# Cross-attention and a top-2 mixture of experts: tile tails in blocks of 32 in place of 64, with copies, a counting product, a table load and the last step moved

## The reference

```python
# x, ctx: (32, 64, 256) float32; attention takes groups of 8 of the 64 rows as heads
x = x + xattn(layernorm(x), ctx, ctx)          # softmax over 256 keys, 8 rows a head
x = x + ffn(layernorm(x), gate, w0, w1, wo)    # 8 experts, 2 of them per token

def ffn(x, gate_kernel, w0_kernel, w1_kernel, wo_kernel):   # EMB 256, MLP 512
    gate_logits = einsum('bsd,de->bse', x, gate_kernel)
    weights, indices = top_k(gate_logits, 2)
    weights = softmax(weights)
    combine = einsum('bsk,bske->bse', weights, one_hot(indices, 8))
    inter = silu(einsum('bsd,edm->bsem', x, w0_kernel)) * einsum('bsd,edm->bsem', x, w1_kernel)
    return einsum('bse,bsem,emd->bsd', combine, inter, wo_kernel)
```

## Time and profile before

| | |
|---|---|
| median of 3 runs | 501.8 us (499.94 to 504.45) |
| the profiled execution | 499.44 us, its span 497.7 us |
| mean granted TensorE clock | 0.928 |
| PE, DVE, ACT, POOL busy | 88%, 57%, 49%, 43% of the span |
| attention, to the last pv product | until about 238 us |
| planning | about 249 to 265 us |
| expert steps | about 268 to 487 us |

### The profile page before, as it was taken

The page is one execution under the profiler, slowest core; times in us unless marked ns, Lnnn a source line. Parts: engine busy times, 40 slices in busy tenths (PEclk is TensorE's granted clock), DMA queues, the critical chain, the costliest instruction groups (busy, mean ns, idle before and its releaser), DMA issues.

```text
span 497.7 us, 10117 instructions
## 1 busy us (share of the span) xinstructions
PE 438.9 (88%) x3288; PEld 225.4 (45%) x3289; DVE 285.8 (57%) x610; ACT 241.5 (49%) x476; POOL 212.1 (43%) x237
## 2 busy tenths in 40 slices
PE   4948998988999988979479999999999999999991
PEld 3412343433443433424234555555656666666650
DVE  7898989898869898866598423242322222222220
ACT  2654888878668879865202233333322222222220
POOL 9564040454554223296403244455463544444222
PEclk9875999999879999986776999999999999999997
DMA  8776569787967762449961022333333322233211
GB/s 242 218 217 168 139 197 221 220 228 212 262 177 200 199 173 87 126 119 393 398 236 42 22 42 43 53 46 50 53 47 50 63 43 42 42 49 50 30 21 21
DMA packets 42341, 65.27 MB, mean 131 GB/s; under 512 B 6330, under 2 KB 32251, under 8 KB 42299
## 3 DMA queue, kind: packets, MB, share of 16 engines
q1 hardware_dynamic: 28570, 38.49, 27.5%
q0 software_dynamic: 11424, 24.12, 20.8%
q10 hardware_dynamic: 2304, 2.10, 1.3%
HBM read 39.79 MB, written 24.58 MB: 129 GB/s over the span
## 4 chain that ended last, share of the span: by engine, by line
PE 52%; issue 19%; POOL 11%; DVE 7%; DMA 3%; ACT 2%; SPq 2%; ACTq 1%; POOLq 0%; DVEq 0%
PE max_ps L1611 22%; PE pv_ps L1633 6%; PE ring_ps L1633 5%; PE pv_ps L1484 3%; PE ring_ps L1570 3%; DVE mx L1001 3%; PE max_ps L1605 3%; PE ring_ps L1467 2%; POOL normed L636 2%; ACT pt L839 2%; PE ring_ps L1560 2%; POOL q_sb L622 2%; POOL num L616 2%; PE ring_ps L1628 2%; SPq L443 1%
## 5 line engine op out<-in xcount | busy, mean ns | idle before, releaser
L1001 DVE TENSOR_REDUCE mx<-max_ps 128x4 f32<-128x1024 f32 x128 | 150.2, 1216 | 19.2 <-PE max_ps L1343 19.1
L839 ACT ACTIVATE pt<-ring_ps 128x512 f32<-128x512 f32 x256 | 139.1, 598 | 32.4 <-PE ring_ps L1467 28.9
L1611 PE MATMUL max_ps<-w_sb,pt 128*128 x256 | 115.4, 593 | 1.0 <-ACT pt L903 0.9
L766 POOL DMA_INDIRECT out<-rb,sidx x36 | 56.8, 1578 | 96.8 <-DVE rb L1319 42.2
L1297 DVE TENSOR_TENSOR pt<-pt,max_ps 128x512 f32<-128x512 f32 x36 | 24.8, 688 | 104.9 <-issue 86.0
L1484 PE MATMUL pv_ps<-pt,w_sb 128*27 128x256 f32 (+2 forms) x1024 | 81.4, 402 | 1.1 <-ACT pt L839 0.5
L1611 PEld LDWEIGHTS max_ps<-w_sb,pt 128*128 128x128 f32 x256 | 46.1, 190 | 47.3 <-issue 47.3
L1467 PE MATMUL ring_ps<-Q,K 50*128 50x256 f16 x512 | 53.2, 288 | 11.6 <-ACT pt L839 8.9
L1343 PE MATMUL max_ps<-K,Q 48*128 48x256 bf16 x512 | 53.4, 289 | 11.0 <-DVE mx L1001 11.0
L910 ACT ACTIVATE pt<-ring_ps 128x512 f32<-128x512 f32 x36 | 21.5, 597 | 68.7 <-PE ring_ps L1570 68.7
L903 ACT ACTIVATE pt<-ring_ps 128x256 f32<-128x256 f32 x36 | 13.8, 384 | 67.1 <-PE ring_ps L1560 44.8
(11 more groups left out here) (216 smaller groups left out, 540.1 us busy)
## 6 DMA issues: line engine op xcount, KB each, us to landing
w_sb<-in_L_ffn_w_kernel POOLq DMA_DIRECT2D x16, 512.0 KB, 10.6
K<-k_img SPq DMA_DIRECT2D x14, 448.0 KB, 6.2
Q<-q_img SPq DMA_DIRECT2D x14, 448.0 KB, 7.7
k_img<-kpart SPq DMA_DIRECT2D x28, 192.0 KB, 3.7
q_img<-qpart SPq DMA_DIRECT2D x28, 192.0 KB, 3.4
wo_sb<-in_L_ffn_wo_kernel POOLq DMA_DIRECT2D x8, 512.0 KB, 12.7
acc<-pvs SPq DMA_DIRECT2D x6, 512.0 KB, 3.1
q_sb<-in_x SPq DMA_DIRECT2D x16, 128.0 KB, 4.1
```

The costliest lines, as they stand in the source:

```text
L766: g.indirect_dma_start(xacc, bass.IndirectOffsetOnAxis(ap=sidx[sl.par][:, 0:1], axis=0), y_sb[sl.par], None, compute_op=ALU.add).then_inc( ...
L839: a.activation(pt[:, (2 * i + h) % PTN, :, :], bank(key)[:, :, :], ACT.Exp, scale=SCALE).then_inc(ring_read, 1)
L1001: v.tensor_reduce(mx[:, t % 2, :, :, p].rearrange("q mt h -> q h mt"), max_ps[n % 2][:, :, :, :], axis=AX.X, op=ALU.max).then_inc(max_read, 1)
L1611: last = nc.tensor.matmul(flat(max_ps[sl.par][:, bank_of]), lhsT=xT[sl.par][:, k * P:(k + 1) * P], rhs=weight(w, e, KC, k), start=(k == 0) ...
```

## The change

`TAILS` becomes (64, 32): GRAIN is 32, PER 4, KINDS 4, NT 34, NMIX 6, and a mixed tile has four blocks and nine copies on each of DVE and ACT. DVE's copies are spread anew: the first w0 block is copied in the step of the mixed tile before, and wo blocks a step sooner. `rank(0)` goes from pair 0 to pair 2 of the last tile. On POOL the first `rsqrt_last` stands ahead of four wo loads. ACT runs a one-column SiLU after the exponential of the gate. In the last step PE puts the output of the tile before between the two halves of `hidden`, and DVE makes its product after scaling. With NT = 34 the loop over plain tiles has no rounds left, so all steps from t = 20 on are written out.

```diff
-    TAILS = (64,)
+    TAILS = (64, 32)
...
-    ranks_at = {(T - 1, 0): 0, (T - 1, 7): 1}
+    ranks_at = {(T - 1, 2): 0, (T - 1, 7): 1}
...
             load_each(load_w0, range(E))
-            load_each(load_wo, range(4, E))
...
             rsqrt_last(0, 2, 1)
+            load_each(load_wo, range(4, E))
             load_each(load_w1, range(3))
...
             a.activation(e2[:, :], gap[:, :], ACT.Exp).then_inc(e2_done, 1)
+            a.activation(mx[:, 0, 0, 0, 0:1], nbias[:, 2:3], ACT.Silu)
...
+            def stage_w0(j, n):
+                e = expert_block(j, n + 1)
+                for k in range(KC):
+                    v.tensor_copy(w0_st[n][:, k, :], w0_sb[:, bass.ds(e * KC + k, 1), :].rearrange("p o f -> p (o f)")
+                                  ).then_inc(w0_copied, 1)
             def stage(sl):
                 n = sl.c % EVERY
+                if sl.peeled and sl.t == 0:
+                    stage_w0(0, 0)
+                if n == EVERY - 1:
+                    if sl.c < AFTER - 1:
+                        stage_w0(sl.j + 1, 0)
+                    return
+                if n + 1 < PER - 1:
+                    stage_w0(sl.j, n + 1)
                 if n < PER - 1:
-                    e = expert_block(sl, n + 1)
-                    for k in range(KC):
-                        v.tensor_copy(w0_st[n][:, k, :], w0_sb[:, bass.ds(e * KC + k, 1), :].rearrange("p o f -> p (o f)")
-                                      ).then_inc(w0_copied, 1)
-                if 0 <= n - 1 < PER - 1:
-                    e = expert_block(sl, n)
-                    v.tensor_copy(wo_st[n - 1][:, 0:FC // 2, :], wo_sb[:, bass.ds(e * FC, FC // 2), :]).then_inc(wo_copied[0], 1)
+                    e = expert_block(sl.j, n + 1)
+                    v.tensor_copy(wo_st[n][:, 0:FC // 2, :], wo_sb[:, bass.ds(e * FC, FC // 2), :]).then_inc(wo_copied[0], 1)
...
+            def multiply(sl):
+                v.wait_ge(sil_done, sl.t + 1)
+                v.wait_ge(h1_full, sl.t + 1)
+                if sl.has(-2):
+                    v.wait_ge(inter_turned, sl.t - 1)
+                v.tensor_tensor(inter[sl.par], sil[sl.par], flat(max_ps[sl.par][:, 1]), ALU.mult).then_inc(inter_done, 1)
...
             def experts(sl):
                 if sl.has(GX):
                     next_gather(sl.at(GX))
-                if sl.has(0):
-                    v.wait_ge(sil_done, sl.t + 1)
-                    v.wait_ge(h1_full, sl.t + 1)
...
-                    v.tensor_tensor(inter[sl.par], sil[sl.par], flat(max_ps[sl.par][:, 1]), ALU.mult).then_inc(inter_done, 1)
+                if sl.has(0) and not (sl.peeled and sl.t == NT - 1):
+                    multiply(sl)
...
+                if sl.peeled and sl.t == NT - 1:
+                    multiply(sl)
                 if not sl.plain and sl.c < AFTER:
                     stage(sl)
...
-            def hidden(sl, e):
+            def hidden(sl, e, halves=(0, 1)):
...
+                if sl.peeled and sl.t == NT - 1:
+                    hidden(sl, e, (0,))
+                    output(sl.at(-1), e_before)
+                    hidden(sl, e, (1,))
+                    return
                 if sl.has(0):
                     hidden(sl, e)
```

More of the change, by code:

```diff
@@ L1251, in next_gather, with expert_block @@
                 v.tensor_copy(gidx[sl.buf][:, :], tokg[:, bass.ds(sl.col, 1)]).then_inc(gidx_done, 1)
-            def expert_block(sl, c):
-                return v.value_load(expert_of[0:1, bass.ds(PER * sl.j + c, 1)])
+            def expert_block(j, c):
+                return v.value_load(expert_of[0:1, bass.ds(PER * j + c, 1)])
+            def stage_w0(j, n):
[3 more added lines that the diff above has]
+                                  ).then_inc(w0_copied, 1)
             def stage(sl):
                 n = sl.c % EVERY
-                if n < PER - 1:
-                    e = expert_block(sl, n + 1)
-                    for k in range(KC):
-                        v.tensor_copy(w0_st[n][:, k, :], w0_sb[:, bass.ds(e * KC + k, 1), :].rearrange("p o f -> p (o f)")
-                                      ).then_inc(w0_copied, 1)
-                if 0 <= n - 1 < PER - 1:
-                    e = expert_block(sl, n)
-                    v.tensor_copy(wo_st[n - 1][:, 0:FC // 2, :], wo_sb[:, bass.ds(e * FC, FC // 2), :]).then_inc(wo_copied[0], 1)
+                if sl.peeled and sl.t == 0:
[6 more added lines that the diff above has]
+                    stage_w0(sl.j, n + 1)
+                if n < PER - 1:
+                    e = expert_block(sl.j, n + 1)
+                    v.tensor_copy(wo_st[n][:, 0:FC // 2, :], wo_sb[:, bass.ds(e * FC, FC // 2), :]).then_inc(wo_copied[0], 1)
             def turned_spares():
@@ L1290, in experts @@
                     next_gather(sl.at(GX))
-                if sl.has(0):
-                    v.wait_ge(sil_done, sl.t + 1)
-                    v.wait_ge(h1_full, sl.t + 1)
-                    if sl.has(-2):
-                        v.wait_ge(inter_turned, sl.t - 1)
-                    v.tensor_tensor(inter[sl.par], sil[sl.par], flat(max_ps[sl.par][:, 1]), ALU.mult).then_inc(inter_done, 1)
+                if sl.has(0) and not (sl.peeled and sl.t == NT - 1):
+                    multiply(sl)
                 if sl.peeled and sl.t == 0:
@@ L1599, in hidden @@
                     pe.wait_ge(w1_copied, (sl.j + 1) * KC * (PER - 1))
-                for w, w_st, bank_of, full in ((w0_sb, w0_st, 0, h0_full), (w1_sb, w1_st, 1, h1_full)):
+                for bank_of in halves:
+                    w, w_st, full = ((w0_sb, w0_st, h0_full), (w1_sb, w1_st, h1_full))[bank_of]
                     if sl.mixed:
```

## The result

The changed kernel takes 487.64 us (median of 4 runs, 486.32 to 488.38) against 502.94 us (4 runs) of the kernel before on the same chip: a ratio of 0.970, 95% interval 0.9645 to 0.9755. The profiled execution took 487.11 us, its span is 485.1 against 497.7. The forecast of 488.5 lies near it, its range holds, and so do most terms of its sum; two terms missed by 0.6 and 0.7 us in opposite directions. One sentence of the forecast was wrong, and it stood beside a term of zero: what I said of the copies.

What follows compares the result with a forecast made beforehand. PE's tile count and time bound the expert stage, with PE stops at attention's end and DVE's planning chain besides. Terms summed to -11.8 us: 487.6 from the profiled time, 490.0 from the median, forecast 488.5, range 484.5 to 494.5.

Steps and rivals of the forecast that it cites:

- Number of tiles: Expert stage: blocks of 32 cut the tiles from 36 to 34, two plain steps of 5.82 us fewer, -11.64 us.
- Mixed tiles: Expert stage: six mixed tiles for four, each 0.66 us over a plain one, column groups side by side; +1.5 us, +1.2 to +3.6.
- Copies: Expert steps: nine copies per group on each of DVE and ACT fit in idle time or behind PE's work, 0 us.
- First step: Start of the expert stage: DVE makes five copies and three register loads for two copies; +0.6 us, bounds 0 and 1.8.
- Planning: DVE's chain after attention: one more kind adds a subtraction, a product and an addition; +0.9 us, bounds 0.6 and 1.9.
- Counting product and power: Last attention tile: PE's 2.39 us idle goes, DVE's chain starts sooner; -3.4 us (-3.9 at full clock, -3.1 at half).
- Table: ACT's sigmoid table load ahead of the first SiLU: moving it gives 0 us, since the first product waited for PE.
- last step split: End of the kernel: the scatter's queue wait goes but the last tile is ready later; +0.2 us, bounds -0.9 and +1.1.
- A: Attention tail gives nothing, PE waits at turn_rows and rank(1) and the clock falls there instead; -8.4 us, 492 us, chance 0.15.
- B: Expert steps: ACT's copies show where three stand ahead of SiLU; +7 us, 495 us, chance 0.07.
- C: Expert stage: scatters become the bound, DVE's copies holding up POOL's descriptors, groups of 25.7 us; +7 us, 495 us, chance 0.07.
- D: Mixed tiles: four column groups don't go side by side, 5.2 us each, +31 us, 519 us, chance 0.04.

Runs made afterwards that it cites:

- e4_copies_late: Changed kernel with DVE's copies put back in the steps where the kernel before made them; 507.92 us, ratio 1.0201 to the kernel before.
- e5_no_split: Changed kernel without the split of the last step; 487.42 us, ratio 0.971 to the kernel before.
- e3_tail_only: Kernel before with only two edits, first counting product at pair 2 and POOL's first power ahead of four wo loads; 495.40 us, ratio 0.9880.
- e6_no_silu: Changed kernel without the one-column SiLU after the exponential that loads the table early; 489.21 us, ratio 0.9752 to the kernel before.
- a1_after: The changed kernel run again with nothing edited, the second repeat; 489.46 us, ratio 0.982 to the kernel before.

## Why the prediction was right, and where not

- *The sum.* The stretches give -12.6 for -11.8. The tail came out 0.6 us better than its term and the mixed tiles 0.7 us worse, and that these two cancel is luck. The whole times are no finer check: their medians differ by 15.3, 10.4 and 11.7 us from the kernel before in the three measurements (490.11 and 489.46 us in the repeats), so that 487.64 falls so near to 488.5 is chance in part. The range covers all three.
- *Number of tiles, -11.64.* Right: 34 products, plain steps 5.82 us.
- *Mixed tiles, +1.5: mis-sized.* From the second product on, the groups with mixed tiles cost 3.52, 0.82, 0.79, 0.81, 0.59 and 0.75 us over a plain group's 23.28, against 3.28, 0.60, 0.60 and 0.60 before (the first group is over 3 us longer in both). That is +2.2 us, where the term of the sum was +1.5. The mechanism held: the four column groups go side by side, in rounds 0.43 us apart as before. PE's timeline of a mixed hidden layer, one round and the start of the next:

```profile
288.44 0.59 PE L1622 MATMUL max_ps<-w_sb,pt 128*32 x1
288.45 0.60 PE L1622 MATMUL max_ps<-Q,pt 128*32 128x512 f32 x2
288.46 0.59 PE L1622 MATMUL max_ps<-K,pt 128*32 128x512 f32 x1
288.87 0.59 PE L1622 MATMUL max_ps<-w_sb,pt 128*32 x1
```

What is dearer than the 0.66 I took is the step with the mixed output: 6.39 us from one `turn_x` to the next (296.15 to 302.54), 6.11 before; why is left open below. Bounds held.
- *Copies, 0: the number right, one reason wrong.* PE had no gap, and ACT's late SiLU ended in the cover I had named. The sentence that failed is "Making the copies a step sooner only gives them more room". It decides the sign of the change: `e4_copies_late` is 17 us slower in the steps and, as a whole, slower than the kernel before. I had looked at whether DVE has room for nine copies in four steps (it has: 2.9 us idle a step) and not at when the last of them is due. With three blocks instead of one, the third w0 block in the old order falls at the end of DVE's step just ahead of the mixed tile, and PE stands at that tile before the copy begins. A cost of zero by idle time says nothing of a deadline.
- *First step, +0.6.* Right, +0.58. DVE's timeline, for the earlier trace rows, shows no wait left ahead of the second product:

```profile
273.18 0.86 DVE L1261 COPY Q<-w_sb 128x512 f32 x2 [1.08 <-issue]
274.39 0.86 DVE L1261 COPY Q<-w_sb 128x512 f32 x2 [0.35 <-issue]
275.60 0.43 DVE L1277 COPY Q<-wo_sb 128x512 f32 x1 [0.34 <-issue]
...
276.00 0.68 DVE L1305 TENSOR_TENSOR pt<-pt,max_ps 128x512 f32<-128x512 f32 x1
```

- *Planning, +0.9.* Right, +0.89.
- *Counting product and power, -3.4.* It came out at -4.0, the value stated for the case that the clock stays up (-3.9), and the two waits that I said would be next are there (0.94 and 1.40 us). In both repeats, though, the clock fell between the two waits, and the tail was still 22.4 to 22.5 us. The case of half clock in the last products came in `e5_no_split`: -2.7 us, for the -3.1 that I had. What I hadn't said is that neither move is worth anything alone.
- *Table, 0* and *last step split, +0.2*: measured 0 and 0.1. For the split the exchange was as worked out, one wait for another.
- *Rivals.* A (the tail gives nothing) fell in the changed kernel; it is what each move alone does. Its fall of the clock at `turn_rows` did come in the repeats, but cost nothing. B fell, though ACT is late in ten steps. C fell: scatters that wait for the one before start 4.5 to 4.9 us apart (4.5 to 4.7 in the kernel before, as in the earlier trace rows), and no group behind the first takes more than 24.10 us, where this rival asked for 25.7. D fell by the starts above.

## What to carry to other kernels

When one engine stands between two others that are both late, undo the moves one at a time: here two moves gave 4 us together, while alone one gave nothing and the other lost 1 us, since the first stop only passed its place on to the next. When work is spread over steps, check the last piece of it against the moment at which it is due, and not only the sum of the work against the sum of the idle time. And read a small effect from stretches between like events; most of them repeated to 0.2 us here, where the runs of one kernel spread by up to 10, but a stretch in which the clock can fall needs more than one profile.

## What was not expected of the hardware

**The same wait sometimes keeps the clock and sometimes loses it.** Seven profiles have the changed tail: three of the changed kernel, and `e3_tail_only`, `e4_copies_late`, `e5_no_split` and `e6_no_silu`. In all of them PE waits 0.81 to 0.94 us at `turn_rows`. In the first profile (0.94) and in `e5_no_split` and `e6_no_silu` (0.81) the granted clock stayed at 1.00 up to the wait at the second count. In the four others (0.84 to 0.94, both repeats among them) it was at half 3 us later, and back at 1.00 before the last products. Windows of `a1_after`:

```profile
225.00:227.00 2.00, 2.00 (x24) 1.26 (x20) 1.93 (x3) 1.35 (x4) 2.00 (x4) 0.74 1.02 383
227.00:229.00 2.00, 2.00 (x20) 0.32 (x12) 1.86 (x11) 1.20 (x3) 0.88 (x2) 0.50 1.03 390
```

It cost nothing there, because PE only waited less at the second count (0.61 to 0.67 us for 1.40). In `e5_no_split` the clock fell with the second wait, with no slack left behind it, and the tail was 1.3 us longer. The length of the first wait alone doesn't tell the two cases apart: 0.94 is among both. A forecast of a stretch with waits like these has to carry both levels.

**Four products started some 10 ns apart.** PE's timeline in a mixed output:

```profile
296.46 0.40 PE L1645 MATMUL ring_ps<-wo_sb,pt 128*32 x1
296.47 0.41 PE L1645 MATMUL ring_ps<-Q,pt 128*32 128x256 f32 x2
296.48 0.40 PE L1645 MATMUL ring_ps<-q_sb,pt 128*32 128x256 f32 x1
296.70 0.38 PE L1645 MATMUL ring_ps<-wo_sb,pt 128*32 x1
```

Four starts lie within 0.02 us, the next four 0.24 us later. The Trainium skill, "TensorE: Matmul & The Clock Gate" (Wait - 56ns, not 53.3ns?), has two matmuls at least about 25 ns apart; the starts in this trace don't show that, for products in different column groups, and the surcharge of 0.6 us that I had estimated from it does not come from the starts.

**The turn behind a mixed output is longer.** From `turn_inter` to the next hidden layer it takes 299.01 - 298.33 = 0.68 us behind a mixed output, against 0.49 in the kernel before, where 16 fewer products stand in the queue ahead; the profile puts the gaps down to issue. The hidden layer behind it is 0.1 us longer as well:

```profile
299.01 3.69 PE L1628 MATMUL max_ps<-w_sb,pt 128*128 x8
...
302.54 0.38 PE L1576 MATMUL ring_ps<-ident,normed 128*128 128x128 f32 x2
```

From its start to `turn_x` that is 3.53 us, where the kernel before has 3.43 (302.02 to 305.45). The two make up the 0.28 us of the step. That PE's sequencer falls behind after a long series of small products would fit, and no run tried it: the cause stays open.

**Some copies and scatters are slower side by side.** DVE and POOL of the changed kernel, in the step behind the first mixed output:

```profile
300.68 1.64 POOL L766 DMA_INDIRECT out<-rb,sidx  x1 [3.82 <-DVE rb L1333]
301.31 0.76 DVE L1277 COPY Q<-wo_sb 128x512 f32 x1 [0.45 <-issue]
```

This copy beside POOL's scatter takes 0.76 us and the scatter 1.64, where 0.43 and 1.57 are usual. It is not the rule: between 280 and 410 us sixteen of DVE's wo copies overlap a scatter, and the fifteen others take 0.43. The scatters are more regular: of nine that start while a pair of w0 copies runs, eight take 1.64 to 1.82 us, and all the others 1.55 to 1.59; in the kernel before, though, one of 1.64 us (at 284.75) stands beside no copy. That would be rival C's mechanism, and is in line with what the Trainium skill says in "SBUF - State Buffer" (SBUF: two separate sides) of a copy that shuts out descriptor writing; no run tried it by itself, and it is too small and too seldom here to reach PE.
